# FFN 1's output bias and a half sum of the dot products move from VectorE to GpSimd, behind a new wait

## What is computed

```python
# layer 0
x = x + L0_conv(ln_c(x))    # per 3x3 patch: similarity to 512 vectors, argmax, small MLP
t = tokens(x); t = t + L0_ffn(ln_t(t))
# layer 1
x = x + L1_conv(ln_c(x))    # local response normalisation over a 5x5 window
t = tokens(x); t = t + L1_ffn(ln_t(t))

# in L0_conv: y[ij] = <patch pixel ij, w_mask[v]> / (norms)
sim_map_max = y[max_ch]     # the nine products of a patch's pixels with the chosen vector
inp = concatenate([integrate, sim_map_max]); h = leaky_relu(inp @ w_i1.T + b_i1) ...

# each FFN
q_mul = round to 5 exponent and 2 mantissa bits; q_acc = round to 5 and 10 (float16)
_qlinear(x, W, b) = q_acc(q_acc(q_mul(x) @ q_mul(W).T) + q_mul(b))
ffn(x) = _qlinear(relu(_qlinear(x, W1, b1)), W2, b2)
```

## Time and profile before

| | |
|---|---|
| median of 3 runs | 3355.06 us (3355.01 to 3362.01) |
| the profiled execution | 3366.41 us |
| its span (first to last instruction) | 3364.6 us |
| DVE busy | 3022.2 us, 90% |
| PE busy | 2824.8 us, 84% |
| ACT busy | 2608.5 us, 78% |
| POOL busy | 1192.6 us, 35% |
| granted TensorE clock, mean | 0.957 |

### The profile page before, as it was taken

The page is one execution under the profiler, slowest core; times in us unless marked ns, Lnnn a source line. Parts: engine busy times, 40 slices in busy tenths (PEclk is TensorE's granted clock), DMA queues, the critical chain, the costliest instruction groups (busy, mean ns, idle before and its releaser), DMA issues.

```text
span 3364.6 us, 55888 instructions
## 1 busy us (share of the span) xinstructions
PE 2824.8 (84%) x15886; PEld 1512.2 (45%) x15886; DVE 3022.2 (90%) x10843; ACT 2608.5 (78%) x7047; POOL 1192.6 (35%) x1159
## 2 busy tenths in 40 slices
PE   5888898988888888888888888888989899889654
PEld 2444444444445444444444444444444445444322
DVE  6888999999999999999999999999999999999532
ACT  0444788888888887878888788888888888888876
POOL 1223243333334333333433433334343434334221
PEclk9999999999999999999999999999999999999755
DMA  3111222222222222232232222223222223232111
GB/s 91 48 55 47 66 69 84 80 72 81 71 73 80 69 83 66 69 82 67 68 84 65 73 79 68 84 68 83 71 82 71 83 70 84 68 84 58 37 48 43
DMA packets 236607, 237.32 MB, mean 71 GB/s; under 512 B 183426, under 2 KB 186764, under 8 KB 236300
## 3 DMA queue, kind: packets, MB, share of 16 engines
q1 hardware_dynamic: 226060, 214.86, 23.2%
q0 software_dynamic: 10240, 18.89, 2.2%
HBM read 134.72 MB, written 57.02 MB: 57 GB/s over the span
## 4 chain that ended last, share of the span: by engine, by line
DVE 36%; ACT 26%; PE 25%; DMA 7%; issue 5%; SPq 0%; POOL 0%; POOLq 0%; DVEq 0%
ACT ffn_hid L552 11%; ACT ffn_x L585 10%; PE banks L415 10%; DVE st L815 7%; DMA ffn_xT<-ffn_x 7%; DVE ffn_hid L911 7%; DVE pix L824 6%; DVE ffn_hid L903 6%; PE banks L392 4%; PE banks L460 4%; PE banks L400 3%; DVE x L894 3%; PE banks L438 2%; ACT h L665 2%; ACT x L598 1%
## 5 line engine op out<-in xcount | busy, mean ns | idle before, releaser
L552 ACT ACTIVATE ffn_hid<-banks 128x512 f16<-128x512 f32 (+1 forms) x2304 | 1052.7, 492 | 387.3 <-PE banks L392 386.6
L415 PE MATMUL banks<-wcT,xc 128*128 128x512 f32 x2304 | 1217.8, 620 | 79.7 <-DVE pix L824 43.6
L392 PE MATMUL banks<-ffn_xT,w1q 128*128 128x512 fp8e5 (+1 forms) x2304 | 706.7, 340 | 260.1 <-ACT ffn_hid L552 170.4
L1080 POOL TENSOR_TENSOR x<-x,ffn_f 128x864 f32<-128x864 f32 x256 | 491.7, 1921 | 1038.5 <-DVE nb L777 920.3
L824 DVE TENSOR_REDUCE pix<-banks 128x1 f32<-128x512 f32 x1152 | 787.1, 684 | 69.0 <-PE banks L415 68.7
L392 PEld LDWEIGHTS banks<-ffn_xT,w1q 128*128 128x128 bf16 x2304 | 219.5, 98 | 783.7 <-ACT ffn_hid L552 541.5
L400 PE MATMUL banks<-w2q,ffn_hid 128*128 128x96 bf16 x6912 | 394.6, 211 | 160.7 <-DVE ffn_hid L911 159.9
L903 DVE TENSOR_SCALAR ffn_hid<-ffn_hid,b1q 128x1152 f16<-128x1152 f16 x768 | 419.3, 559 | 116.0 <-ACT ffn_hid L552 116.0
L400 PEld LDWEIGHTS banks<-w2q,ffn_hid 128*128 128x128 f16 x6912 | 353.1, 101 | 364.1 <-issue 335.0
L598 ACT ACTIVATE x<-x,cols 128x96 f32<-128x96 f32 x1152 | 511.7, 473 | 0.0
L585 ACT ACTIVATE ffn_x<-x,cols 128x96 fp8e5<-128x96 f32 x1152 | 501.4, 485 | 0.0
(11 more groups left out here) (137 smaller groups left out, 2849.9 us busy)
## 6 DMA issues: line engine op xcount, KB each, us to landing
xt<-x_tok_in SPq DMA_DIRECT2D x128, 432.0 KB
xc<-x_chan_in SPq DMA_DIRECT2D x128, 432.0 KB
out_tok<-x SPq DMA_DIRECT2D x128, 432.0 KB
ffn_xT<-ffn_x SPq DMA_TRANSPOSE x256, 2.6
win<-x_tok_in,xrow POOLq DMA_INDIRECT x128, 3.1
wrow<-vector_table,vidx POOLq DMA_INDIRECT x128, 2.7
shift<-shift_in SPq DMA_DIRECT2D x1, 960.0 KB
vector_table<-wtab SPq DMA_DIRECT2D x1, 384.0 KB, 2.9
```

Of the source, the lines that this page charges most:

```text
L392: last = pe.matmul(bank[:, 0:c1 - c0], w1q[:, ffn.layer, c * P:(c + 1) * P], pairs, start=True, stop=True)
L415: last = pe.matmul(ps_score[score_bank(j)], xc[p][:, j, :], wcT[:, :], start=True, stop=True)
L552: return nc.scalar.activation(dst, src, ACT.Copy)
L1080: tt(dst, x, ffn.f[:, :, :], ALU.add).then_inc(ready, 1)
```

## The change

VectorE no longer adds FFN 1's bias; GpSimd does it, behind the x2 sum and ahead of the gather. GpSimd adds the upper 48 channels of the product to the lower 48 (half_dot, 128x432), and VectorE's dots reduction reads that half. FFN 0's bias stays on VectorE. GpSimd waits for FFN 1's rounding (`hid_ready`) before the product, in steps that have an FFN 1 tile.

```diff
+        half_dot = sb("half_dot", [P, J, C // 2])
@@ VectorE, mlp_input
-                f3c.add(nc.vector.tensor_reduce(dots[:, :], prod_dot[:, :, :], AX.X, ALU.add),
+                f3c.add(nc.vector.tensor_reduce(dots[:, :], half_dot[:, :, :], AX.X, ALU.add),
@@ VectorE, body
                 run(roots_of, 1)
-                ffn_bias(ffn1, k.rtail, x4_ready)
                 run(roots_of, 2)
@@ GpSimd, dot_product
-                tt(prod_dot[:, :, :], xt[:, f2 & XT - 1], unit, ALU.mult).then_inc(prod_dot_ready, 1)
+                tt(prod_dot[:, :, :], xt[:, f2 & XT - 1], unit, ALU.mult).then_inc(dot_chain, 1)
+                pool.wait_ge(dot_chain, f2 + 1)
+                tt(half_dot[:, :, :], prod_dot[:, :, 0:C // 2], prod_dot[:, :, C // 2:C],
+                   ALU.add).then_inc(prod_dot_ready, 1)
+
+            def ffn_bias(ffn, tile, added):
+
+                pool.wait_ge(ffn.taken, (tile + 1) * UNITS + 2)
+                wait_past(pool, added, tile)
+                b2 = b2q[:, ffn.layer, :].rearrange("p (o c) -> p o c", o=1).broadcast_to([P, J, C])
+                tt(ffn.f[:, :, :], ffn.y[:, :, :], b2, ALU.add).then_inc(ffn.f_ready, 1)
@@ GpSimd, body
                     ffn_output(ffn0, k.tail, x1[k.q][:, :, :], x2[:, k.tail & RING - 1], x2_ready)
+                if k.rtail is not None:
+                    ffn_bias(ffn1, k.rtail, x4_ready)
                 if k.f2 is not None:
                     gather(k.f2)
@@
                 if k.f2 is not None:
+                    if k.rear is not None:
+
+                        pool.wait_ge(ffn1.hid_ready, k.rear + 1)
                     dot_product(k.f2)
```

More of the change, by code:

```diff
@@ L255, in build @@
         vidx_ready, wrow_loaded = sem("vidx_ready"), sem("wrow_loaded")
-        prod_dot_ready, inp_ready = sem("prod_dot_ready"), sem("inp_ready")
+        dot_chain, prod_dot_ready, inp_ready = sem("dot_pool_chain"), sem("prod_dot_ready"), sem("inp_ready")
         f3_chain = sem("f3_vector_chain")
```

## The result

The changed kernel takes 3394.09 us (median of 4 runs, 3388.28 to 3399.41) against 3355.72 us (median of 4, 3355.01 to 3362.01): ratio 1.0104, 95% interval [1.0089, 1.0119], 1.0% slower. The forecast was 3390 us, the range 3322 to 3428.

The account below looks back on a forecast made before the run. VectorE was taken to bound only each step's second half. Plain +35, collision -38, window +15, LRN +20, end +1 gave +33 us on the profiled 3366.4, 3399; as median 3390 us, 1.0% slower, range 3322 to 3428.

Parts of the forecast that it names:

- What bounds the step: VectorE has slack in the step's first half; in the second, from 11.6 to 23.08 us, delays lengthen the step one to one.
- Collisions: In 28 steps GpSimd's product starts before FFN 1's rounding and blocks it; the wait ends that, -38 us net.
- Half sum and x4 over the ReLU: Half sum of 1.03 us pushes x4 onto FFN 0's first ReLU: 0.6 us per step, +35 us in 58 plain steps.
- Window steps: In the 14 steps making window parts, the later x4 covers sim: +1.1 us each, +15 us.
- LRN steps: In 14 steps with LRN columns: 1.0 us saved, 1.7 lost behind the bias, 0.7 at the ReLU; +20 us.
- Bias elsewhere: FFN 1's bias on GpSimd lies in the first half, covered: 0 in plain, collision and window steps; add about 1.82 us.
- First 13 steps: At the start of the run VectorE waits for TensorE several times, so the change was worth 0.
- Profile against median: Runs' median is 11 us below the profiled execution: recorder's cost gives 3388, fewer collision steps 3399; 3390 taken.
- A: Rival: FFN 0's first ReLU is not hit; only repairs and LRN saving stay, -69 us, about 3290; chance 0.16.
- B: Rival: half the price, 0.3 us at FFN 0's first ReLU; -15 us, 3340 to 3352, near no change; chance 0.13.
- D: Rival: VectorE is the bound after all, so 1.0 us is saved in each of 114 steps; 3197 us; chance 0.04.
- C: Rival: FFN 1's transposition becomes the next bound, landing 0.4 us late in 86 steps; +34 us more, 3424; chance 0.12.

Follow-up runs that it names:

- save_only: wait_only with FFN 1's bias left out altogether and dots over half the channels, no work added to GpSimd; 3296.33 us, ratio 0.9817.
- quarter_sum: Changed kernel with a GpSimd sum of 24 channels and dots over these 24, half of the product left out; 3343.06 us, ratio 0.9954.
- half_only: wait_only plus the half sum on GpSimd, FFN 1's bias staying on VectorE; 3372.38 us, ratio 1.0028.
- wait_only: Kernel before with only GpSimd's product waiting for FFN 1's rounding; bias and dots stay on VectorE; 3320.97 us, ratio 0.9876.
- bias_only: wait_only plus FFN 1's bias on GpSimd, no half sum, dots over all 96 channels; 3341.93 us, ratio 0.9945.
- x4_early: wait_only with GpSimd's x4 sum moved right behind x2, ahead of the gather, except in LRN steps; 3320.84 us, ratio 0.9896.
- sum_twice: Changed kernel with GpSimd making the half sum twice, the first into a tile nobody reads; 3444.45 us, ratio 1.0260.
- x4_early_half: half_only with the x4 sum moved behind x2, ahead of the gather, except in LRN steps; 3323.14 us, ratio 0.9889.
- no_wait: Changed kernel without GpSimd's new wait for FFN 1's rounding; 3468.13 us, ratio 1.0313.

## Why the prediction was right, and where its sizes were off

- **What bounds the step**: right. save_only shows the first half to be slack (0.95 us less, nothing gained), quarter_sum and half_only the second half to pass everything on (0.46 us for 0.47).
- **Collisions**: right in kind and number; -34.1 for -38 us. (The prediction's 47 us over 1.78 is 26, not 27; the roundings lost 48.0 us, 1.71 for each of the 28.) What I had not seen is why there were 28: I took the late landings for a small remainder (0.05 us), while they made the collisions and stay when these go (23.65 in wait_only). In the changed kernel most of that is gone: its transposition is issued earlier against the step, 20 of the 27 landings with the packet there take under 4.05 us, and the steps with and without it take 23.94 and 23.90 us.
- **Half sum and x4 over the ReLU**: right. Sum 1.11 us for 1.03, time left 0.84 for 0.78, price 0.66 for 0.6: 0.07 x 86 = 6 us. The rest lies in single steps: the 86 steps of the changed kernel are 14 us over 86 x 23.75. Of these, 8 are in six steps in which the granted clock falls to 0.50 in the first half; steps of 25.41 us are of this kind, and TensorE's 128x512 matmuls (L416) take 1.06 us or more instead of 0.59 there. 5 are in 13 steps whose transposition lands more than 3.25 us into the step. The prediction had no term for the clock.
- **Window steps**: mechanism right, term mis-sized: +6.0 for +15. Sim takes 1.75 us (+1.05, as forecast), but the ReLU ahead of it shrank from 1.29 to 0.83: it starts at 2668.11, 0.51 us before the product's end, where it was 0.98 us. I had counted what x4 newly covers and left in place what the product no longer does.
- **LRN steps**: right, +18.9 for +20, and the single terms hold when steps at full clock are compared. L940 waits 1.78 us as foreseen. The saving is 0.84 us (save_only) for the 1.0 I took; the bias costs 1.15 (bias_only) where my terms give 1.7 - 0.5 = 1.2; the half sum costs 0.35 (half_only) for 0.7 - 0.5 = 0.2; all together 28.05 - 26.54 = 1.51 for 1.4. The means don't show it: by them bias_only loses 1.42 us and half_only gains 0.25, for a stretch at clock 0.50 stands in 12 LRN steps of the one which are 1.1 us longer than its others, and in 5 of the other, which are as long as its others. The Trainium skill (SBUF — State Buffer, Who interferes with whom) says that a VectorE instruction with two SBUF inputs contends with a GpSimd instruction that reads SBUF; L940's 1.78 us is the case that stood open in the prediction, and the trace agrees.
- **Bias elsewhere**: right, 0 in plain and window steps (bias_only: 23.33 against 23.32, 24.75 against 24.85), under the cover of the gather's wait for vidx. An f16 add costs GpSimd the 1.82 us of the f32 one.
- **First 13 steps**: 0 predicted, -7.3 measured. They take 304.9 us before, 301.7 with the wait alone, 297.5 in the changed kernel and 293.6 in x4_early and save_only, with and without relief. The time follows TensorE's clock: the granted clock is 0.50 for 47.8 us of these steps before, 37.5 with the wait alone, 34.1 in the changed kernel, 23.9 in save_only and 17.1 in x4_early, and over the 14 traces the two go together (correlation 0.91). Which causes which, and why the clock fell less often, stays open.
- **Profile against median**: the profiled execution of the changed kernel equals its median, and the kernel before had medians from 3355.7 to 3362.0 beside the experiments, with single runs up to 3369.7. So the 11 us between its profile and its median lie within its own spread and need no cost of the recorder.
- **The total**: that the parts add up to +27.7 for +33 us is in part luck, since they are off by +8, +4, -9, -1 and -7.

Of the rivals, A and B fell with the ReLU's 1.16 us, D with save_only; C costs the changed kernel some 5 us and is large only in sum_twice. The best kernel of those that compute the whole result is the wait alone, 0.9876 [0.9860, 0.9893]: the rest of the change costs 73 us on top of it (77 by the ratios). x4_early and x4_early_half are not to be told from it.

## What to carry to other kernels

Work moved from VectorE to GpSimd is not free when GpSimd is idle: list which VectorE operations (here the two-input ones, the ReLU, the rounding) will lie beside the moved one and beside everything queued behind it, and price each by the time left. The place of an operation counts more than its length: the same instructions cost 3372 us in one order and 3323 in another. Take a change apart before judging it; here one wait was worth -1.2% and was hidden in a change of +1.0%. And before a mean over steps is explained, set apart the steps in which the granted clock was lower: here that settled what the sums alone left open.

## What was not expected of the hardware

- Tiny operations pay the whole wait: sim (128x9) took 1.75 us instead of 0.15 and L940 (128x72) 1.78 instead of 0.23.
- The engine that starts first, even by 0.06 us, pays nothing, and the other waits almost to its end: the ReLU 0.50 and x4 2.11 us in sum_twice, the rounding 2.74 and the product 2.02 in no_wait. FFN 0's first ReLU paid 0.18 or 0.19 us less than the time that GpSimd's operation had left, each time: 0.79 of 0.98, 0.66 of 0.84, 0.33 of 0.51.
- A 16,384-byte code packet that starts less than 2.2 us behind a transposition's issue goes with a landing of at least 4.06 us instead of a median of 2.6, in 227 of 227 cases in 14 kernels. It drifts slowly against the step, so its harm comes in long stretches and looks like a property of the step.
- GpSimd: 128x864 f16 with a broadcast operand 1.82 us, 128x432 f32 1.11, 128x216 0.65.
